# Two layers, one core: the way in and out of a head attention reordered, and the dense units' first layer begun inside it

## The reference

```python
x = x + L0_xattn(layernorm(x), ctx)
x = x + L0_ffn(layernorm(x))                       # 8 experts, top 2, SwiGLU
# head attention, 16 heads of 64; mask (B, 512, 1601)
dots = einsum('bhid,bhjd->bhij', q @ Wq, ctx @ Wk) * 64 ** -0.5
attn = softmax(where(mask, -max, dots))
x = x + einsum('bhij,bhjd->bhid', attn, ctx @ Wv) @ Wo + bo
# dense units: the last block
xf = layernorm(x)
tw, ti = top_k(softmax(xf @ router_w + router_b), 8)
x = x + sum_e cw_e * (silu(xf @ w1_e + b1_e) @ w2_e + b2_e) + sum_s (silu(xf @ sw1_s + sb1_s) @ sw2_s + sb2_s)
```

## Time and profile before

| what | value |
|---|---|
| median of 3 runs | 1468.39 us |
| the profiled execution, its own time | 1472.92 us |
| its span in the trace | 1471.2 us |
| TensorE matmul busy | 1399.7 us (95%) |
| VectorE busy | 1021.7 us (69%) |
| ScalarE busy | 778.5 us (53%) |
| GpSimd busy | 294.8 us (20%) |
| experts of the first layer end (last L1308) | at 507.4 us |
| head attention | 507 to 1001 us |
| dense units | 1002.7 us to the end |

### The profile page before, as it was taken

One profiled execution on the slowest core, in us unless ns is written; L12 is line 12 of the kernel. 1 busy time (PEld: TensorE's weight loads), 2 busy tenths in 40 slices (PEclk: granted clock), 3 DMA queues, 4 the chain that ended last, 5 costly groups with the idle time before them and its releaser, 6 DMA issues.

```text
span 1471.2 us, 27431 instructions
## 1 busy us (share of the span) xinstructions
PE 1399.7 (95%) x9946; PEld 1117.6 (76%) x9946; DVE 1021.7 (69%) x2459; ACT 778.5 (53%) x1681; POOL 294.8 (20%) x331
## 2 busy tenths in 40 slices
PE   6899998998999879999999999988999999999998
PEld 5898997885556556666667666657889999999997
DVE  6767773565657668877877787776487766777753
ACT  4556663334766467677877777763442232222221
POOL 0000001242254322300000000023233333233321
PEclk9999999999999989999999999989999999999999
DMA  9432201323555111100000000002036544555431
GB/s 348 138 111 68 82 15 55 119 87 111 172 182 178 43 46 31 37 13 2 16 23 20 13 30 2 2 1 63 1 74 150 131 101 110 129 125 115 103 100 55
DMA packets 78479, 117.80 MB, mean 80 GB/s; under 512 B 7487, under 2 KB 51845, under 8 KB 77829
## 3 DMA queue, kind: packets, MB, share of 16 engines
q1 hardware_dynamic: 75269, 107.59, 26.0%
q0 software_dynamic: 3072, 8.39, 1.8%
HBM read 97.09 MB, written 18.87 MB: 79 GB/s over the span
## 4 chain that ended last, share of the span: by engine, by line
PE 58%; DVE 4%; issue 2%; ACT 1%; DVEq 0%; ACTq 0%
PE PS L68 13%; PE PS L69 13%; PE PS L70 13%; PE PS L2600 6%; PE PS L2573 6%; PE PS L2587 3%; PE PS L2615 3%; DVE c_sm L2809 1%; DVE c_pr L2818 1%; ACT c_pr L2689 1%; PE PS L1895 0%; DVE st L360 0%; DVE c_u L2822 0%; PE PS L388 0%; DVE c_k L2787 0%
## 5 line engine op out<-in xcount | busy, mean ns | idle before, releaser
L1968 ACT ACTIVATE d_hf<-PS,C 128x512 f32<-128x512 f32 x160 | 109.1, 691 | 262.1 <-PE PS L70 260.4
L2698 ACT ACTIVATE c_pt<-PS 100x512 f32<-100x512 f32 x256 | 139.0, 595 | 97.5 <-PE PS L2587 97.4
L953 POOL CAST d_h<-d_hf 128x512 fp32r<-128x512 f32 x160 | 128.1, 813 | 303.9 <-DVE d_hf L2050 248.4
L68 PE MATMUL PS<-d_w,d_h 128*128 128x256 f32 x640 | 182.1, 285 | 1.4 <-issue 1.4
L70 PE MATMUL PS<-d_w,d_h 128*128 128x256 f32 x640 | 179.8, 281 | 0.0
L69 PE MATMUL PS<-d_w,d_h 128*128 128x256 f32 x640 | 179.8, 281 | 0.0
L2689 ACT ACTIVATE c_pr<-c_sm,c_mn 128x400 f32<-128x400 f32 x256 | 158.7, 626 | 20.1 <-DVE c_mn L2809 20.1
L2809 DVE CUSTOM_DVE_ANT_0 c_sm<-PS,c_mw 128x400 f32<-128x400 f32 x256 | 136.2, 570 | 21.3 <-PE PS L2573 17.6
L958 DVE TENSOR_TENSOR d_h<-d_hf,d_h 128x512 fp32r<-128x512 f32 x160 | 131.8, 881 | 13.2 <-POOL d_h L953 13.2
L2050 DVE TENSOR_TENSOR d_hf<-d_hf,d_wb 128x512 f32<-128x512 f32 x128 | 89.8, 709 | 71.0 <-ACT d_hf L1968 70.5
L2573 PEld LDWEIGHTS PS<-c_k,c_q 64*128 64x128 f32 x768 | 63.0, 189 | 85.8 <-issue 49.6
(11 more groups left out here) (304 smaller groups left out, 3139.5 us busy)
## 6 DMA issues: line engine op xcount, KB each, us to landing
d_wb<-wscratch SPq DMA_DIRECT2D x64, 512.0 KB, 7.5
a_cT<-ctxT SPq DMA_DIRECT2D x4, 1601.0 KB, 8.0
a_raw_nat<-ctx SPq DMA_DIRECT2D x4, 1536.0 KB
zs<-e_zero SPq DMA_DIRECT2D x2, 2944.0 KB, 23.0
ys<-e_y SPq DMA_DIRECT2D x46, 128.0 KB, 1.8
d_w1r<-l_w SPq DMA_DIRECT2D x10, 512.0 KB, 4.1
d_w2r<-l_w SPq DMA_DIRECT2D x10, 512.0 KB, 5.2
e_z<-zs SPq DMA_DIRECT2D x9, 512.0 KB, 4.3
```

Source lines behind the costliest of these rows:

```text
L68: pe.matmul(out, w[0], x[0], start=first, stop=False)
L953: i = eng.tensor_copy(mem["h"][b % 2][0][:, m, :], mem["hf"][:, m, :])
L1968: act.activation(memD["hf"][:, m, :], PS[:, m, :], ACT.Silu, bias=C[:, b1 + g * 4 + m:b1 + g * 4 + m + 1]).then_inc(DM["act"], 1)
L2698: act.activation(c_pt[u % 2][0:KW, :, :, i * P + r * DH:i * P + (r + 1) * DH].rearrange("p h t q -> p (h t) q"), PS[0:KW, BT + r, :].rearr ...
```

## The change

*Way in.* Of batch 1's layernorm the scaling `ln_scale` moves from q 42 to q 45, behind all SwiGLU work; its transposes, copies and remainders leave the expert loop and stand in the opening of the head attention, in banks 3 and 7. The opening issues scores(1) before values(2), keys(1) and queries(1), and VectorE and ScalarE do keys(1), queries(1) and the normalisation of step 1 ahead of the loop. ScalarE begins with an exponential of one column, which nothing reads.

*Way out.* `d_hidden` and `d_silu` become functions of their own. TensorE makes parts 0 and 1 of unit 0 in the last step of u 31 and parts 2 and 3 in the last step of u 32; the Silu of parts 0 and 1 stands in u 32 on ScalarE. `d_pe` begins with hidden(1). The remainders of the first unit's weights go from GpSimd to VectorE (`d_first_low`), at steps 126 and 128. GpSimd waits for the last project before it leaves the window path. Batch 3's layernorm moves behind unit 0's remainders on VectorE and behind unit 0's copies on GpSimd.

```diff
@@ mb_pe, tick (mb_act likewise at q 38 and 44)
-                for b in range(2):
-                    if q == (37, 43)[b]:
-                        pe.wait_ge(SP_["planned"], PLAN[1] + PL)
-                        for j in range(2):
-                            ln_turn(pe, 2, b, j, 6 + j)
+                if q == 37:
+                    pe.wait_ge(SP_["planned"], PLAN[1] + PL)
+                    for j in range(2):
+                        ln_turn(pe, 2, 0, j, 6 + j)
...
@@ mb_dve, tick
-                if q == 42:
+                if q == 45:
                     ln_scale(dve, 2, 1)
-                if q == 45:
-                    for j in range(2):
-                        ln_low(dve, 2, 1, j, 6 + j)
...
         def d_first_pool(pool):
             pool.wait_ge(DM["w_in"], 32)
             pool.tensor_copy(memD["w1"][0][0][:, :, :], memD["w1r"][:, :, :]).then_inc(DM["w1_hi"], 1)
             pool.tensor_copy(memD["w2"][0][0][:, :, :], memD["w2r"][:, :, :]).then_inc(DM["w2_hi"], 1)
-            pool.wait_ge(DM["w1_hi"], 1)
-            pool.tensor_tensor(memD["w1"][0][1][:, :, :], memD["w1r"][:, :, :], memD["w1"][0][0][:, :, :].bitcast(F32),
-                               ALU.subtract).then_inc(DM["w_lo"], 1)
...
+        def d_first_low(dve, layer):
+            dve.wait_ge(DM[f"w{layer}_hi"], 1)
+            dve.tensor_tensor(memD[f"w{layer}"][0][1][:, :, :], memD[f"w{layer}r"][:, :, :],
+                              memD[f"w{layer}"][0][0][:, :, :].bitcast(F32), ALU.subtract).then_inc(DM["w_lo"], 1)
...
@@ d_pe
             def second(u):
                 pe.wait_ge(DM["h_lo"], u * 4 + 4)
+                if u == 0:
+                    pe.wait_ge(DM["w_lo"], 2)
+                    pe.wait_ge(attn_done, 1)
...
-            hidden(0)
             for u in range(DU):
                 if u + 1 < DU:
-                    hidden(u + 1)
+                    d_hidden(pe, u + 1)
                 second(u)
...
@@ w_pe, opening
             queries(0)
+            for j in range(2):
+                ln_turn(pe, 2, 1, j, (BT + 1, BY + 1)[j])
             scores(0)
             values(1, 0)
+            scores(1)
             values(2, 0)
             keys(1)
             queries(1)
-            scores(1)
...
@@ w_pe, loop, i == 3
                     elif u + 2 < UNITS:
                         keys(u + 2)
                         queries(u + 2)
+                    elif u >= UNITS - 1 and u <= UNITS:
+                        pe.wait_ge(F["min"], 2 * QT * UNITS)
+                        if u == UNITS:
+                            pe.wait_ge(F["t_out_act"], 2 * QT * UNITS)
+                        d_hidden(pe, 0, range(2) if u == UNITS - 1 else range(2, 4))
...
@@ w_act
+            act.activation(c_l[:, 3, 0:1], ident[:, 0:1], ACT.Exp)
             high_keys(0)
             high_queries(0)
+            for j in range(2):
+                ln_high(act, 2, 1, j, (BT + 1, BY + 1)[j])
...
+                    if i == 0 and u == UNITS:
+                        d_silu(act, 0, range(2))
...
@@ w_pool, its last line
+            pool.wait_ge(F["y"], UNITS)
...
@@ w_dve, opening
             masked(0)
+            ln_low(dve, 2, 1, 0, BT + 1)
             values_out(1)
-            values_out(2)
             masked(1)
             normalised(0)
+            ln_low(dve, 2, 1, 1, BY + 1)
+            values_out(2)
+            normalised(1)
+            low_keys(1)
+            low_queries(1)
...
@@ w_dve, loop
+                    if s == QT * UNITS - 2:
+                        d_first_low(dve, 1)
+                    if s == QT * UNITS:
+                        d_first_low(dve, 2)
```

More of the change, by code:

```diff
@@ L1867, in d_pe @@
         def d_pe(pe):
-            def hidden(u):
-                g, b = u // B, u % B
-                if b == 0:
-                    pe.wait_ge(DM["w_lo"], g * 2 + 2)
-                if g == 0:
-                    pe.wait_ge(LN["lo"], (3 * B + b) * 2 + 2)
-                for m in range(4):
-                    wait_past(pe, DM["act"], (u - 1) * 4 + m + 1)
-                    for k in range(KD):
-                        last = split_matmul(pe, PS[:, m, :], [w[:, k, m * P:(m + 1) * P] for w in memD["w1"][g % 2]],
-                                            [ZT[:, b, h, k, :] for h in range(2)], k == 0, k == KD - 1)
-                    last.then_inc(DM["h"], 1)
             def second(u):
@@ L1964, in d_act @@
                 g, b = u // B, u % B
-                for m in range(4):
-                    act.wait_ge(DM["h"], u * 4 + m + 1)
-                    wait_past(act, DM["h_lo"], (u - 1) * 4 + m + 1)
-                    act.activation(memD["hf"][:, m, :], PS[:, m, :], ACT.Silu,
-                                   bias=C[:, b1 + g * 4 + m:b1 + g * 4 + m + 1]).then_inc(DM["act"], 1)
+                d_silu(act, u, range(2, 4) if u == 0 else range(4))
                 if u == 0:
@@ L2711, in w_act @@
             exponentials(1)
+            high_keys(1)
+            high_queries(1)
             for u in range(UNITS + 1):
@@ L2896, in g_pe @@
         def g_pe(pe, m, F):
+            for j in range(2):
+                ln_turn(pe, 2, 1, j, 6 + j)
             pe.wait_ge(x_done[1], B * 8)
@@ L2902, in g_pe @@
             ln_pe(pe, 3, batches=range(B - 1))
+            d_hidden(pe, 0)
         def g_act(act, m, F):
+            for j in range(2):
+                ln_high(act, 2, 1, j, 6 + j)
             act.wait_ge(PF["lo"], len(EARLY))
@@ L2909, in g_act @@
             ln_act(act, 3, batches=range(B - 1))
+            d_silu(act, 0, range(2))
         def g_dve(dve, m, F):
+            for j in range(2):
+                ln_low(dve, 2, 1, j, 6 + j)
             dve.wait_ge(PF["lo"], len(EARLY))
@@ L2918, in g_dve @@
             ln_dve(dve, 3, batches=range(B - 1))
+            for layer in (1, 2):
+                d_first_low(dve, layer)
         def g_pool(pool, m, F):
```

49 lines of the change are left out of this document (31 added, 18 removed).

## The result

| | runs | median, us | range, us |
|---|---|---|---|
| kernel before | 4 | 1468.44 | 1465.25 to 1469.49 |
| changed kernel | 4 | 1457.52 | 1456.24 to 1458.43 |

The ratio is 0.9929, with a 95% interval of 0.9911 to 0.9946: the change is worth 10.9 us in medians. Between the two profiled executions it is 14.6 us (1472.92 and 1458.33). The forecast was 1452.5, with 15.9 us of gain. Where the 5 us between forecast and median went is the question of the experiments.

The account below looks back on a forecast made before the run. With TensorE 95% busy, only its stands and half-clock time could be won: 4.0 + 0.8 + 2.6 + 6.2 + 2.3 = 15.9 us off the 1468.4 us median gives 1452.5 us, range 1447 to 1461.

Parts of the forecast that it names:

- Terms 1 and 2: Expert tail: earlier SwiGLU, shorter product, full-clock matmuls, 4.0 us; from there to step 0's scores at full clock, 0.8 us.
- term 4: Unit 30: remainders on VectorE remove TensorE's 4.06 us stand and 2.1 us of slow clock; 6.2 us, bounds 4.1 to 6.5.
- term 5: Drain: unit 0's 24 matmuls cover waits of 0.84 and 1.42 us; 2.3 us gain, bounds 0 and 2.3.
- Term 3: Opening, step 0 to step 6: reordering saves 2.6 us despite a new 3.2 us stand; bounds 0 to 5.1.
- the saving is in microseconds of stalls and carries over: Whole kernel: 15.9 us, summed from the 1472.92 us profile, is subtracted unchanged from the 1468.4 us median.
- The first rival: Opening: worth nothing, through two clock drops or later masks, gathers and transfers; 1455.9 us, chance 0.15.
- a sign of being wrong: Start of unit 0's second layer: second(0) waiting on VectorE's `d_h`, where 0.7 us of slack was forecast.
- The rival of GpSimd late at the exit: Attention exit: GpSimd over 4.6 us late; mild form 1455.5 us, chance 0.07; hard form 1473 us, chance 0.02.

Follow-up runs that it names:

- second profile: The kernel before, unedited, profiled once more; this profiled execution took 1469.33 us.
- remainders only: Kernel before with only the two remainders of the first dense unit's weights moved to VectorE, steps 126 and 128; median 1465.25 us, ratio 0.9968.
- way in only: Kernel before with only the expert-loop and opening edits, drain and remainders as before; median 1465.05 us, ratio 0.9970.
- the changed kernel's second: The changed kernel run and profiled once more, unedited; median 1457.49 us, ratio 0.9921 to the kernel before.
- second half behind the exit: Changed kernel with parts 2 and 3 of unit 0's first layer put back behind the exit; median 1461.06 us.
- drain only: Kernel before with only unit 0's first layer in the drain and batch 3's layernorm moved; median 1467.79 us, ratio 0.9983.

## Why the prediction was right or wrong

The direction was right, and so were the places and causes of terms 1, 2 and 4 and of the two filled waits of term 5. Term 3 gave hardly anything. The sum was 4 to 5 us too large, and that it was no more is in part luck: term 5 gave 1.3 us more than forecast, from the stand at the jump, which the forecast had kept as it was. Means of the table's columns, against the terms:

| term of the forecast | forecast | from the profiles |
|---|---|---|
| 1 and 2, to the scores of step 0 (A) | 4.8 | 15.62 - 11.62 = 4.0 |
| 3, step 0 to step 6 (B) | 2.6 | 26.50 - 26.18 = 0.3 |
| 4, remainders on VectorE (D) | 6.2 | 13.69 - 9.80 = 3.9 |
| 5, drain (E) | 2.3 | 30.40 - 26.84 = 3.6 |
| sum | 15.9 | 11.8 |

(A: four profiles with the old order and the nine with the new, all of these between 11.48 and 11.65; B: the same four, against the five with the change's opening and scaling; D: four with GpSimd's subtractions beside the normalisations, seven with VectorE's; E: four of the old exit, six of the new without a further edit there.) The medians gave 10.9 and 11.4.

**The step that was off** is the sentence "the saving is in microseconds of stalls and carries over", and beside it term 3 took one fall of the clock where often two came, and term 4 took the wait before step 126 to stay as it was. The first profile took 1472.92 us where the four runs recorded with it lay between 1465.25 and 1469.49, and its surplus over the second profile, 3.9 us from A to E, lay in the very stalls that the forecast added up.

- *Term 4* took the whole 4.06 us for gone. That wait was 1.83 or 1.84 us in three other profiles, and the wait before step 126 is 2.00 us now, where the first profile had 1.24. The waits before steps 125 and 126 together were 5.30, 4.04, 3.07 and 3.58 us with the old order, 4.0 in the mean, and are 2.0 in all seven profiles of the new: 2.0 us gone, and not 4.06. The other 1.9 of the 3.9 us are work at full clock instead of half, near the 2.1 of the forecast, although half clock still came in three of the eight profiles that have the 2.0 us wait before step 126 and no subtraction of GpSimd's ahead of it. The forecast had named a fall of the clock all the same as its lower bound, 4.1 us, and remainders only gave 4.4.
- *Terms 1 and 2* counted 0.7 and 0.8 us for the end of half clock behind the wait of 2.60. In two of the four profiles with this wait there was none (A of 14.93 and 14.90, against 16.30 and 16.35). With full clock both before and after, A falls by 3.3 us. What the runs added is that the wait of 0.95 is followed by full clock in all nine.
- *Term 3.* Its course was right up to the last step: the wait for `values(2)` ended 5.95 us behind the scores of step 0 (forecast 6.2), the scores of step 5 came at 18.69 (18.2), with one fall of the clock. It failed at two places. The row it started from, 27.28 us, was the longest of four (mean 26.50), which is 0.8 of the missing 2.3 us. And where it forecast 27.3 - 2.6 = 24.7 us, the five profiles have 26.18 in the mean, 1.5 more: in three of them (way in only, the changed kernel's second, second half behind the exit) half clock also came behind the new stand for `values(2)`, a second drop, which the forecast had as its lower bound. The windows of the changed kernel's second profile:

```profile
510.00:515.00 5.00, 2.17 (x11) 1.37 (x9) 3.14 (x10) 1.72 (x6) 3.78 (x5) 0.86 0.44 120
515.00:520.00 5.00, 5.00 (x37) 4.18 (x35) 2.48 (x6) 1.10 (x2) 4.05 (x5) 0.80 0.35 105
```

  The waits were in part only moved (6.31 us against 6.79). The first rival, the opening worth nothing, is nearer to what was measured than the term: way in only gave 4.6 us, of which A has 4.0.
- *Term 5* had the two waits right, 2.26 us. It said "the 2.39 us at the jump stay"; they fell to 0.73, a gain of 1.66, and 0.55 of it went into the wait of second(0) on VectorE's `d_h`, which the forecast had named as a sign of being wrong. The medians of drain only (0.7 to 4.3 us) can't tell 2.3 from 3.6.

The rival of GpSimd late at the exit did not come. The trace shows no gap of GpSimd there: its first copy starts at 992.18, less than 0.3 us behind the last project's end. The Trainium skill, "Runtime: NRT & Kernel Launch", section Instruction fetch mechanics, has a taken branch out of the fetched pages stall the engine until the target is there; no run here shows such a stall on GpSimd, and on TensorE the stand is 2.3 us in one order of the work and 0.7 in the other, across the same jump.

## What to carry to other kernels

A stall that is read from one profile has to be seen in a second, if possible on another chip, before its length goes into a sum, above all where two engines collide or the clock falls behind it. In a prologue or a drain, write down for each engine which of its next two instructions the bounding engine waits for first, and put that one first; the order that is right there can be wrong in the steady state, where it cost 50 us. Where a wait can't be removed, work that was due soon anyway goes into it, as twelve matmuls went into each wait of the drain and keys and queries into that of the opening.
